# Batch period 0 entered earlier, gathering on GpSimd, a later weight split and a twelve-batch loop body in a decoder layer

## The reference

```python
x = layernorm(x + self_attention(x, wq, wk, wv))          # one head, softmax over queries, upper triangle
x = layernorm(x + cross_attention(x, ctx, Wq.., Wo, bo))  # 16 heads of 8, 1500 keys a batch
x = layernorm(x + moe(x, Wr, W1, W2))                     # 8 experts, top 2, capacity 560, 128 -> 512 -> 128, relu
```

## Time and profile before

| | |
|---|---|
| median of 3 runs | 948.24 us (946.95 to 949.38) |
| the profiled execution | 953.25 us, of which its span is 951.2 us |
| mean granted TensorE clock | 0.974 |
| TensorE busy | 906.0 us (95% of the span) |
| VectorE busy | 725.0 us (76%) |
| ScalarE busy | 628.6 us (66%) |
| GpSimd busy | 350.9 us (37%) |

### The profile page before, as it was taken

One profiled execution on the slowest core, in us unless ns is written; L12 is line 12 of the kernel. 1 busy time (PEld: TensorE's weight loads), 2 busy tenths in 40 slices (PEclk: granted clock), 3 DMA queues, 4 the chain that ended last, 5 costly groups with the idle time before them and its releaser, 6 DMA issues.

```text
span 951.2 us, 28492 instructions
## 1 busy us (share of the span) xinstructions
PE 906.0 (95%) x10439; PEld 744.7 (78%) x10439; DVE 725.0 (76%) x1490; ACT 628.6 (66%) x1081; POOL 350.9 (37%) x336
## 2 busy tenths in 40 slices
PE   6779999999999999999999999999998899999995
PEld 4647788878788887778888877788776778999894
DVE  6666777777777777777777777778878667777997
ACT  3646777777777677777777777777665444445554
POOL 6452352233343322333332233333220431113992
PEclk9888999999999999999999999999989899999998
DMA  6538566666555666665566666655546001002331
GB/s 145 118 81 201 127 151 148 143 145 140 121 121 128 147 147 145 143 138 121 121 130 148 147 144 146 134 121 121 123 99 143 24 2 45 23 23 102 117 116 42
DMA packets 36457, 111.30 MB, mean 117 GB/s; under 512 B 8323, under 2 KB 18885, under 8 KB 36293
## 3 DMA queue, kind: packets, MB, share of 16 engines
q1 hardware_dynamic: 36404, 110.64, 51.2%
HBM read 32.23 MB, written 1.89 MB: 36 GB/s over the span
## 4 chain that ended last, share of the span: by engine, by line
PE 87%; DVE 6%; ACT 2%; issue 2%; SPq 1%; DMA 1%; POOL 0%; ACTq 0%; DVEq 0%
PE psum L1428 18%; PE psum L1611 17%; PE psum L1666 13%; PE psum L1435 8%; PE psum L1440 8%; PE psum L1670 4%; PE psum L1693 3%; PE psum L1694 2%; PE psum L1695 2%; PE psum L1706 2%; PE psum L1705 2%; PE psum L1707 2%; DVE arena L946 1%; SPq L395 1%; DVE K_st L1085 1%
## 5 line engine op out<-in xcount | busy, mean ns | idle before, releaser
L946 DVE TENSOR_REDUCE arena<-psum 128x1 f32<-128x500 f32 x672 | 436.0, 674 | 160.2 <-PE psum L1428 154.2
L759 ACT ACTIVATE arena<-psum 125x896 f32<-125x896 f32 x384 | 334.3, 915 | 127.2 <-PE psum L1611 63.3
L1428 PE MATMUL psum<-K_hi,Q_bd 128*128 128x500 f32 x672 | 290.1, 471 | 9.5 <-DVE arena L946 4.5
L547 POOL TENSOR_TENSOR arena<-arena,K_hi 128x500 fp32r<-128x500 f32 x96 | 119.8, 1249 | 386.9 <-ACT K_hi L690 386.9
L1611 PEld LDWEIGHTS psum<-Q_st,K_st 103*125 103x125 f32 x1536 | 210.9, 190 | 14.9 <-issue 3.5
L1611 PE MATMUL psum<-Q_st,K_st 103*125 103x224 f32 x1536 | 216.7, 276 | 0.0
L1428 PEld LDWEIGHTS psum<-K_hi,Q_bd 128*128 128x128 f32 x672 | 124.3, 193 | 58.2 <-DVE arena L946 38.8
L1666 PE MATMUL psum<-arena 125*25 125x168 f32 x3072 | 160.1, 311 | 0.4 <-issue 0.3
L813 ACT ACTIVATE K_st<-psum 128x448 fp32r<-128x448 f32 x128 | 69.7, 544 | 80.9 <-PE psum L1695 79.3
L1670 PE MATMUL psum<-arena 125*9 125x56 f32 x3072 | 109.3, 214 | 0.0
L1435 PEld LDWEIGHTS psum<-WvA,arena 97*125 97x125 f32 x768 | 102.9, 194 | 4.7
(11 more groups left out here) (253 smaller groups left out, 1021.9 us busy)
## 6 DMA issues: line engine op xcount, KB each, us to landing
K_st<-K_hi SPq DMA_DIRECT2D x256, 187.5 KB, 4.7
K_st<-arena SPq DMA_DIRECT2D x128, 187.5 KB, 3.4
arena<-in_ctx SPq DMA_DIRECT2D x32, 562.5 KB, 6.7
arena<-gate_rows SPq DMA_DIRECT2D x8, 896.0 KB, 4.4
arena<-in_L_ffn_W SPq DMA_DIRECT2D x16, 256.0 KB, 3.1
arena<-OS_all SPq DMA_DIRECT2D x12, 168.0 KB, 4.3
x_rows<-x_all SPq DMA_DIRECT2D x1, 896.0 KB, 6.8
out<-x_all SPq DMA_DIRECT2D x4, 224.0 KB, 3.1
```

Source lines behind the costliest of these rows:

```text
L547: g.tensor_tensor(low.bitcast(F32R), low, K_hi[:, par, n * KB:n * KB + KB].bitcast(F32), ALU.subtract).then_inc(F["keys_low"], 1)
L759: a.activation(P2[c % NP].rearrange("p (n k) -> p n k", n=2), psum[0:CK, 2 + 2 * (c % 2):4 + 2 * (c % 2), 0:HQ // 2], ACT.Exp)\
L946: v.reduce_max(mx[:, par, n // NB, n % NB:n % NB + 1], bank_of(n)[:, 0:KB], AX.X).then_inc(F["piece_max_taken"], 1)
L1428: mm(bank_of(n)[:, 0:KB], Q_bd[:, par].rearrange("p h q -> p (h q)")[:, 128 * (n // NB):128 * (n // NB) + 128], K_hi[:, par, (n % NB) * KB ...
```

## The change

It has four parts. The order of TensorE, VectorE, ScalarE and SyncE around the start of period 0 is another: of batch 1 only pieces 0 and 1 are made ahead of the period, pieces 2 to 20 in it, by tables of its own (`FIRST_EARLY`, `FIRST_MID`, `FIRST_LATE`; a number n stands for batch n // 21, piece n % 21); values (1,0) are made ahead of the last queries, values (1,1) in slot 0, the output weights in slot 1; SyncE issues the keys of batch 1 ahead of the queries of quads 1 to 3 and of x1. Gathering of quads 0 to 2 goes from VectorE to GpSimd (five instructions each, at the end of GpSimd's periods 28 to 30), with a semaphore of its own. GpSimd splits the weights of expert 0 behind the low part of x of quad 0 and waits for the second `scaled`, and TensorE crosses quad 1 in slot 4 instead of 3. The loop has two turns of twelve periods (2 to 25), and 26 to 32 are written out.

```diff
+FIRST_EARLY = {0: (23, 24), 1: (26, 27), 2: (28, 29), 3: (31, 32), 4: (33, 34), 5: (35, 36), 6: (38, 39), 7: (40, 41), 9: (44,), 10: (46,), 11: (47,)}
+FIRST_MID = {7: (42,), 9: (45,), 11: (48, 49)}
+FIRST_LATE = {0: (25,), 2: (30,), 5: (37,), 7: (43,), 11: (50,)}
...
-            with eng.Fori(1, B // 2 - 2) as i:
-                for par in range(2):
-                    period(i * 2 + par, par, i)
-            for b in range(B - 4, B + 1):
+            with eng.Fori(0, 2) as i:
+                for j in range(2, 14):
+                    period(i * 12 + j, j % 2, i * 6 + j // 2)
+            for b in range(B - 6, B + 1):
                 period(b, b % 2, b // 2)
...
+            if isinstance(b, int) and b == 0:
+                return [divmod(n, PIECES) for n in tables[1].get(c, ())]
+            return [(2 if n < NEXT else 1, n) for n in tables[0].get(c, ())]
...
 SyncE
-            sp.wait_ge(S1["queries_split"], NQ)
-            ... (the loads of the queries of quads 1 to 3)
-            sp.dma_start(x1_rows, x1_all[:]).then_inc(x1_saved, 16)
             def period(b, par, half):
                 if has(b, 1):
                     ...
                     load_keys(1 - par, (2, 0, 1))
+                if isinstance(b, int) and b == 0:
+                    sp.wait_ge(S1["queries_split"], NQ)
+                    ... (the same loads)
+                    sp.dma_start(x1_rows, x1_all[:]).then_inc(x1_saved, 16)
...
 GpSimd
+            def gather(n):
+                into, other, third = [OS_all[:, s, tokens(n)] for s in range(SLOTS - 1)]
+                rows = [slot_rows[:, s:s + 1].to_broadcast([128, QC]) for s in range(SLOTS - 1)]
+                pool.wait_ge(w_ev, 3)
+                pool.wait_ge(F["outputs_scaled"], (n + 1) * (B // NQ) + PRIME)
+                step(g.tensor_tensor(into, into, rows[0], ALU.mult))
+                step(g.tensor_tensor(other, other, rows[1], ALU.mult))
+                step(g.tensor_tensor(into, into, other, ALU.add))
+                step(g.tensor_tensor(third, third, rows[2], ALU.mult))
+                g.tensor_tensor(into, into, third, ALU.add).then_inc(S3["quads_gathered"], 1)
...
+                if isinstance(b, int) and B - 5 < b < B - 1:
+                    gather(b - (B - 4))
...
+            low_inputs(passes[0], 0)
+            pool.wait_ge(S3["normed"], 2 + PRIME)
             pool.wait_ge(F["scores_made"], (B - 1) * NC + PRIME)
             split_weights(passes[0], 0)
-            low_inputs(passes[0], 0)
...
 ScalarE
+            values_copy(1, 1, 0)
             query_copy(3)
             keep_extremes(0)
-            values_copy(1, 1, 0)
-            values_copy(1, 1, 1)
...
+                    if isinstance(b, int) and b == 0 and c == 0:
+                        values_copy(1, 1, 1)
...
 VectorE
-            for n in range(max(BEFORE_TURN - 1, 0), BEFORE_TURN + 2):
+            for n in range(max(BEFORE_TURN - 1, 0), BEFORE_TURN):
                 piece_max(1, 1, n)
...
+                    if isinstance(b, int) and b == 0 and c == 1:
+                        output_weights()
...
-                    if isinstance(b, int) and b in (B - 4, B - 3, B - 2) and c in (2, 4, 7):
-                        ...
-                        gathered(P, (2, 4, 7).index(c), tokens(b - (B - 4)))
...
 TensorE
+            pe.wait_ge(F["keys_copied"], 2 * NB + PRIME)
+            value_project(1, 0)
             first_query(3)
             pieces1(*range(BEFORE_TURN))
             turn(0, True)
-            pieces1(BEFORE_TURN)
-            ... (output weights, pieces 3 to 8 of batch 1, value_project(1, 0) and (1, 1))
...
-                        if c == 3:
+                        if c == 4:
                             crossed(P, 1)
...
+                    if isinstance(b, int) and b == 0:
+                        if c == 0:
+                            pe.wait_ge(F["values_copied"], NB + 1 + PRIME)
+                            value_project(1, 1)
+                        if c == 1:
+                            output_weights()
```

More of the change, by code:

```diff
@@ L288, in decoder_kernel @@
         S3 = {n: sem("s3_" + n) for n in (
-            "attended", "gathered", "projected", "projected_copied", "outputs_made", "residual_added", "variance_ready", "rstd_ready", "normed",
+            "attended", "quads_gathered", "gathered", "projected", "projected_copied", "outputs_made", "residual_added", "variance_ready", "rstd_ready", "normed",
             "normed_transposed", "normed_copied")}
@@ L297, in decoder_kernel @@
         gates_out = sem("gates_out")
-        total3 = dict({n: NQ for n in S3}, gathered=NQ + 1)
+        total3 = dict({n: NQ for n in S3}, gathered=2, quads_gathered=NQ - 1)
         total4 = dict({n: 1 for n in S4}, x_split=NQ, counted=ROUNDS, total_made=ROUNDS, weights_high=NE, weights_split=NE,
@@ L332, in total, with pieces @@
             return bank[Y_BANK[n]][0:TT, D * t:D * t + D]
-        def pieces(c, table):
-            return [(2 if n < NEXT else 1, n) for n in table.get(c, ())]
+        def pieces(b, c, tables):
+            if isinstance(b, int) and b == 0:
+                return [divmod(n, PIECES) for n in tables[1].get(c, ())]
+            return [(2 if n < NEXT else 1, n) for n in tables[0].get(c, ())]
         def bank_of(n):
@@ L403, in period @@
                     load_keys(1 - par, (2, 0, 1))
+                if isinstance(b, int) and b == 0:
+                    sp.wait_ge(S1["queries_split"], NQ)
+                    others = outputs_place[:, 0:(NQ - 1) * FIRST_WORDS].rearrange("p (n w) -> p n w", w=FIRST_WORDS)
+                    for q, o in enumerate((HIGH_AT, LOW_AT, HIGH_AT)):
+                        for g in range(HG):
+                            sp.dma_start(Qs_all[32 * q:32 * q + 32, g, QC:B * S].rearrange("p (n c) -> p n c", c=QC), others[32 * g:32 * g + 32, :, o:o + QC]).then_inc(D_["qr"], 16)
+                    sp.dma_start(x1_rows, x1_all[:]).then_inc(x1_saved, 16)
                 if has(b, 3):
@@ L985, in _, with output_weights @@
             row_out(0, 0)
-            for n in range(max(BEFORE_TURN - 1, 0), BEFORE_TURN + 2):
+            for n in range(max(BEFORE_TURN - 1, 0), BEFORE_TURN):
                 piece_max(1, 1, n)
[L988 to L994, removed]
+            def output_weights():
+                dve.wait_ge(w_ps, 2)
+                v.tensor_copy(WoP[:], bank[6][:, 0:256].rearrange("p (s c) -> p s c", s=2))
+                v.tensor_copy(slot_rows[:], bank[6][:, 256:256 + SLOTS - 1]).then_inc(w_ev, 1)
+                dve.wait_ge(w_ev, 3)
+                v.memset(bank[6], 0.0).then_inc(F["bank_cleared"], 1)
             def taken(b, par, c, table):
-                for ahead, n in pieces(c, table):
+                for ahead, n in pieces(b, c, table):
                     if not has(b, ahead):
@@ L1003, in period @@
                 for c in range(NC):
-                    taken(b, par, c, EARLY_PIECES)
-                    taken(b, par, c, MID_PIECES)
+                    taken(b, par, c, (EARLY_PIECES, FIRST_EARLY))
+                    taken(b, par, c, (MID_PIECES, FIRST_MID))
+                    if isinstance(b, int) and b == 0 and c == 1:
+                        output_weights()
                     if c == ROW_SLOT and has(b, 1):
@@ L1033, in period @@
                                                R_sb.rearrange("p (s q) -> p s q", s=SLOTS), ALU.mult, ALU.mult, accum_out=chk_all[:, bass.ds(b - 1, 1)]).then_inc(F["outputs_scaled"], 1)
-                    taken(b, par, c, LATE_PIECES)
+                    taken(b, par, c, (LATE_PIECES, FIRST_LATE))
                     P, norms = passes[0], passes[0].base3["rstd_ready"]
-                    if isinstance(b, int) and b in (B - 4, B - 3, B - 2) and c in (2, 4, 7):
-                        if c == 2:
-                            dve.wait_ge(F["outputs_scaled"], (b - (B - 4) + 1) * (B // NQ) + PRIME)
-                        gathered(P, (2, 4, 7).index(c), tokens(b - (B - 4)))
                     if isinstance(b, int) and b == B - 2:
@@ L1532, in _, with output_weights @@
             turn(0, True)
-            pieces1(BEFORE_TURN)
[L1534 to L1547, removed]
+            def output_weights():
+                pe.wait_ge(S1["queries_copied"], NQ)
+                for s in range(SLOTS - 1):
+                    mm(bank[6][:, 0:128], perm[:, s, :], w_sb["xWo"][:], start=(s == 0), stop=(s == SLOTS - 2))
+                mm(bank[6][:, 128:256], perm[:, SLOTS - 1, :], w_sb["xWo"][:], start=True, stop=True)
+                for s in range(SLOTS - 1):
+                    last = mm(bank[6][:, 256 + s:257 + s], perm[:, s, :], ones[:, 0:1], start=True, stop=True)
+                last.then_inc(w_ps, 1)
             def bank_free(b, kind, n):
@@ L1568, in project @@
             def project(P, n):
-                pe.wait_ge(P.S3["gathered"], n + 1 + (n == NQ - 1) + P.base3["gathered"])
+                if P.past:
```

(11 more changed lines are left out.)

## The result

The change takes 942.96 us (median of 5 runs, 940.24 to 944.15) against 948.64 (5 runs); the ratio is 0.9942, with a 95% interval of 0.9926 to 0.9959. The forecast was 936, a gain of 12; the measured gain is 5.7. The direction and the range held, the size did not.

What follows compares the result with a forecast made beforehand. TensorE bounds the kernel (87% of the chain), so only its idle or lower-clock time can be won. 5.2 + 6.7 + 3.5 + 1.9 - 2.5 = 14.8; 953.25 - 15 = 938.4, taken as 936 given the lower median; range 926 to 944.

Steps and rivals of the forecast that it cites:

- Part 4: Loop of twelve batches a turn: eleven of twelve jumps go, 1.9 us gained; the remaining jump's fetch costs 2.5.
- The base: Start of the sum: profiled execution 953.25 us, median 948.24; how much of the 5.0 between them carries over.
- profiling: Reading of the 5.0 us between profile and median: if due to profiling, all carries over, giving 933.
- a race: Other reading: the collision at 684.49 is avoided in timed runs, 4.5 us of gain not available, giving 937.9.
- Part 1: Head: period 0 begins behind the first row of maxima; 7.7 us gained, 2.5 back by the clock, 5.2 net.
- Part 2: Periods 28 to 30: gathering on GpSimd ends VectorE's collision and TensorE's idle time; 5.4 + 0.9 + 0.4, 6.7 us gained.
- Part 3: Period 31: later split of weights and crossing at slot 4 shorten VectorE's scaling; 3.5 us gained, floor 1.5.
- B: Rival, 17%: tail and jump end worse, the collision absent or gathering over copies, jump costs 5.5; gain 7 to 8, 941.
- C: Rival, 6%: TensorE's code streaming in periods 2 to 25; a late fetch each period makes it slower, 962 at 1.2 us.

Runs made afterwards that it cites:

- e6: The kernel before with gathering on GpSimd alone; 943.57 us, ratio 0.9945 to the kernel before.
- e7: The kernel before with the early period 0 (new head) alone; 945.14 us, ratio 0.9961 to the kernel before.
- e8: The kernel before with the later split of weights and the crossing of quad 1 in slot 4 alone; 944.33 us, ratio 0.9962.
- e2: The change with the loop of before, two periods a turn; 934.15 us, ratio 0.9856 to the kernel before.
- e12: The change with two periods a turn and other tables, fewer pieces of batch 1 side by side in period 0; 934.48 us, ratio 0.9826 to before.
- e3: The kernel before with the change's loop of twelve periods a turn alone; 959.10 us, ratio 1.0111 to the kernel before.
- e5: The kernel before, unchanged, run again for a second profile; 949.02 us, ratio 0.9996.
- e1: The change with all periods written out, no loop and no jump; 935.12 us, ratio 0.9868 to the kernel before.
- e9: The change with two periods a turn on TensorE and twelve on the four other engines; 948.59 us, ratio 0.9978 to before.

## Why the forecast of the size was wrong

**Part 4 is the step that failed.** It read the row rightly: the small body is not fetched again, and 0.17 us a jump are won. It also named what could go wrong, "its one jump may wait for a fetch". But it set the price at 2.5, between 0 and 5.5, with no row near it. Measured in the trace it is 9.2 us around batch 14 and 0.8 in period 26, net of 2.0 for the jumps 8.0; by the ratios 8.2, where the forecast had +0.6. That is 7.6 us, more than the 7.0 by which 936 was missed. I had counted one fetch on one engine. There are two waits on TensorE, 6.46 us together, and the lower clock for 6.8 us; VectorE, whose body no longer stays either, waits beside it.

**The base.** I took the gain from one profile with more of the lower clock than most executions have and carried half of the difference over. My choice between "profiling" and "a race" was a choice between two wrong reasons; it was the clock. The whole gain of 14.8 taken off the median would have been 933.4. The 2.6 us up to 936 had a wrong reason and were luck: without them the miss would have been 9.6 us. They also hid that parts 1 to 3 gave less in the median than the 15.4 forecast, 12.5 by e6, e7 and e8 and 13.7 by e2.

**Part 1, right in mechanism, perhaps too large.** 5.2 forecast, 3.7 by e7 (2.5 to 5.0). Over all profiled executions it is 5.4: period 1 starts at 98.6 us in the mean of six with the old head, at 93.2 in the seven with the new one. The scores began 0.2 us behind the row of maxima (L982 ends at 62.78), and the wait of L688 for the keys is gone. Period 0 took 29.6 us, where 26.3 + 2.5 were forecast. Of the 6.6 us by which period 1 starts earlier in the trace, 2.1 lie ahead of the row of maxima (its end is at 62.78, before at 64.83); little was changed there, but the clock was lower for 13.6 us in this stretch before and for 10.2 in the change, which can be worth up to 1.7 of it. In e7, with the same head and 13.6 us of the lower clock, the row ends at 64.05. In period 0 the clock was lower for 3.4 us only, not for the six forecast, and the period still took longer. So the waits for VectorE were larger than the 1.5 that I had: e12 takes 1.45 out of them.

**Part 2, right in mechanism.** 6.7 forecast by the profile, 6.7 found there; 5.2 by e6, since the 6.8 us of lower clock behind the stall belonged to that profile: in e3, e5 and e7 period 28 took 25.1 to 25.2, not 26.52. Periods 28 and 29 are 21.05 each in the change. GpSimd's five instructions and the stacking behind them:

```profile
685.62 0.93 POOL L560 TENSOR_TENSOR OS_all<-OS_all,slot_rows 128x448 f32<-128x448 f32 x1
686.63 0.93 POOL L561 TENSOR_TENSOR OS_all<-OS_all,slot_rows 128x448 f32<-128x448 f32 x1
687.65 1.16 POOL L562 TENSOR_TENSOR OS_all<-OS_all 128x448 f32<-128x448 f32 x1
688.88 0.93 POOL L563 TENSOR_TENSOR OS_all<-OS_all,slot_rows 128x448 f32<-128x448 f32 x1
689.89 1.14 POOL L564 TENSOR_TENSOR OS_all<-OS_all 128x448 f32<-128x448 f32 x1
691.00 1.69 POOL L540 TENSOR_TENSOR Q_bd<-Qt_all,head_rows 128x896 fp32r<-128x896 f32 x1
```

5.4 us a quad, and nobody waits for them; VectorE's row of maxima beside it (685.71) took its usual 1.10, and none of its maxima was longer.

**Part 3, right.** 3.5 forecast, 3.6 by e8. VectorE, GpSimd and TensorE of the change in period 31, answering to the earlier trace rows:

```profile
738.62 1.94 DVE L896 TENSOR_SCALAR x_all<-x_all,arena 112x128 f32<-112x128 f32 x4
743.11 1.16 DVE L1056 SCALAR_TENSOR_TENSOR OS_all<-arena 128x224 f32<-128x224 f32 x1
...
740.64 1.04 POOL L614 TENSOR_TENSOR K_st<-arena,ones 128x512 fp32r<-128x512 f32 x1 [0.68 <-DVE x_all L896]
...
740.91 0.70 PE L1633 MATMUL psum<-Q_st,K_st 103*125 103x224 f32 x4 [0.57 <-ACT arena L778]
```

The scaling takes 1.94, in the forecast range of 1.1 to 2.2, and TensorE waits 0.57, for the exponentials, where it waited 2.40. The split now lies over L1056 (1.16 instead of 0.4), which nobody waits for.

**The rivals.** B came nearest in the time, 941, and for half of its reason: the jump, which cost more than the 5.5 it gave it. C, a late fetch in every period, is refuted: 22 of the 24 periods of straight code are 21.0 to 21.05 in e1. But the sentence against it, that the straight periods "show no such wait", overlooked a row of my own: period 1 of the kernel before took 21.76.

## What to carry to other kernels

A longer loop body was not a cheaper loop here. Look first whether the instruction queues fetch anything during the turns: where they didn't, a jump cost next to nothing (0.17 us), and one jump to code that was no longer there cost as much as fifty of these. So keep the body as small as it is, on TensorE and on VectorE. And before a gain is summed from one profile, compare its mean granted clock with that of the timed executions: an idle time of 1.8 us was followed by 0, 3.4 or 6.8 us at half the clock in five executions of the same stretch (before, e3, e5, e7, e8).

## What was unexpected of the hardware

The four other engines' jumps out of reach slowed the kernel more without TensorE's than with it: VectorE waited 4.25 and 5.86 us for its code when TensorE's was at hand (e9), and the kernel lost 11.6 us against e2 by the ratios, while all five jumping together lost 8.2. Straight code has rare hiccups too: period 1 of every kernel here, with 21.4 to 21.8 us instead of 21.0, and two later periods of e1 at 21.53 and 21.65. In most of them TensorE has a short idle time of 0.2 to 0.36 us whose end is "issue"; in period 1 of five of the kernels and in period 17 of e1 there is none of this size, so the cause stays open.
